# First attention: output parts made pair by pair in a tensor of their own; two output tiles begun in its last pair

## The reference, cut to what matters

```python
qkv = (x @ W_qkv + b_qkv).reshape(b, n, 3, H, D)
q, k, v = (qkv[0], qkv[1], qkv[2])
phi_q = jax.nn.relu(jnp.einsum('bhnd,md->bhnm', q * scale, random_features))
phi_k = jax.nn.relu(jnp.einsum('bhnd,md->bhnm', k * scale, random_features))
kv = jnp.einsum('bhnm,bhnd->bhmd', phi_k, v)
attn = jnp.einsum('bhnm,bhmd->bhnd', phi_q, kv) / M
out = jnp.transpose(attn, (0, 2, 1, 3)).reshape(b, n, c)
return out @ W_proj + b_proj
```

## Time and profile before

| | us |
|---|---|
| median of 3 runs | 1965.44 (1964.88 to 1968.22) |
| profiled execution, its own time | 1962.91 |
| profiled execution, its span | 1961.1 |
| PE busy in it | 1878.2 (96%) |
| DVE busy | 1204.4 (61%) |
| ACT busy | 873.4 (45%) |

### The profile page before, as it was taken

The page is one execution under the profiler, slowest core; times in us unless marked ns, Lnnn a source line. Parts: engine busy times, 40 slices in busy tenths (PEclk is TensorE's granted clock), DMA queues, the critical chain, the costliest instruction groups (busy, mean ns, idle before and its releaser), DMA issues. The chain is left out here.

```text
span 1961.1 us, 32305 instructions
## 1 busy us (share of the span) xinstructions
PE 1878.2 (96%) x13051; PEld 1771.1 (90%) x13051; DVE 1204.4 (61%) x1895; ACT 873.4 (45%) x1176; POOL 94.4 (5%) x96
## 2 busy tenths in 40 slices
PE   5899899999999999998999999899999999999999
PEld 4899799999999999998899999798878888888899
DVE  8467785444333445446557777665666668889732
ACT  6456521222211212224477752424555557777620
POOL 0000000000000000000000100001111101100000
PEclk9999999999999999999999999899999999999999
DMA  3311244121211122110211041425877779999831
GB/s 92 98 46 36 64 115 111 58 72 41 57 57 57 52 69 62 49 49 22 85 33 33 17 154 41 160 89 185 270 240 237 222 227 335 367 378 377 293 118 40
DMA packets 157962, 250.53 MB, mean 128 GB/s; under 512 B 11949, under 2 KB 86189, under 8 KB 157460
## 3 DMA queue, kind: packets, MB, share of 16 engines
q1 hardware_dynamic: 152532, 231.21, 35.5%
q0 software_dynamic: 5040, 17.56, 3.6%
q10 hardware_dynamic: 272, 0.07, 0.0%
HBM read 228.80 MB, written 20.01 MB: 127 GB/s over the span
## 5 line engine op out<-in xcount | busy, mean ns | idle before, releaser
L183 PE MATMUL psum<-products_room 128*128 128x512 f32 (+2 forms) x2160 | 457.8, 366 | 3.2 <-DVE re_credit L3733 2.0
L183 PEld LDWEIGHTS psum<-products_room 128*128 128x128 f32 (+1 forms) x2160 | 388.8, 188 | 47.3 <-issue 2.4
L183 PE MATMUL psum<-ring_hi,xt_sb 128*128 128x256 f32 (+3 forms) x1920 | 354.9, 283 | 9.6 <-PEq L1290 2.8
L3630 DVE TENSOR_TENSOR products_room<-moe_raw,products_room 128x1536 fp32r<-128x1536 f32 x179 | 312.3, 1754 | 77.4 <-ACT products_room L3529 77.0
L3529 ACT ACTIVATE products_room<-moe_raw 128x1536 fp32r<-128x1536 f32 x179 | 266.0, 1489 | 156.2 <-PE psum L183 85.6
L183 PEld LDWEIGHTS psum<-ring_hi,xt_sb 128*128 128x128 f32 (+1 forms) x1920 | 299.5, 188 | 11.4 <-issue 6.3
L183 PE MATMUL psum<-ring_lo,xt_sb 128*128 128x256 f32 (+3 forms) x960 | 270.2, 282 | 0.0
L183 PEld LDWEIGHTS psum<-ring_lo,xt_sb 128*128 128x128 f32 (+1 forms) x960 | 180.2, 188 | 0.0
L183 PE MATMUL psum<-ring_hi,gnn_sb 128*128 128x256 f32 (+1 forms) x810 | 147.5, 283 | 4.5 <-DVE gnn_sb L1191 3.6
L139 DVE TENSOR_TENSOR ring_lo<-ring_raw,ring_hi 128x1536 fp32r<-128x1536 f32 (+1 forms) x64 | 119.4, 1866 | 50.5 <-ACT ring_hi L128 50.4
L191 PE MATMUL psum<-xt_sb,ring_hi 128*128 128x314 f32 x744 | 140.0, 310 | 0.3
(11 more groups left out here) (529 smaller groups left out, 2752.2 us busy)
## 6 DMA issues: line engine op xcount, KB each, us to landing
moe_raw<-in_L_ffn_Wg_r SPq DMA_DIRECT2D x60, 768.0 KB, 5.9
moe_raw<-in_L_ffn_Wu_r SPq DMA_DIRECT2D x60, 768.0 KB, 5.9
moe_raw<-in_L_ffn_Wd_r SPq DMA_DIRECT2D x60, 768.0 KB, 8.6
ring_raw<-in_L_gnn_w_rel SPq DMA_DIRECT2D x18, 896.0 KB, 5.1
ring_raw<-in_L_mix_W_qkv SPq DMA_DIRECT2D x24, 384.0 KB, 4.2
ring_raw<-in_L_gnn_w_rel SPq DMA_DIRECT2D x9, 768.0 KB, 4.7
ring_raw<-in_L_gnn_w_root SPq DMA_DIRECT2D x6, 896.0 KB, 5.1
count_total_dram<-gnn_sb POOLq DMA_DIRECT2D x3, 1570.0 KB, 11.3
```

What stands on the lines that cost most here:

```text
L183: mm = pe.matmul(out, lhs[a], rhs[b], start=(first and i == 0), stop=(last and i == 2))
L3630: dve.tensor_tensor(wlo[:, i % RING, :], raw[i % RAWS], whi[:, i % RING, :].bitcast(F32), ALU.subtract)\
```

## The change

The values of the first attention no longer have a tensor of their own. A new tensor `hidden_sb` (`k.hb`) lives from the start of the program to the end of the graph convolution; it holds first the values, head by head, and then, from its beginning, the parts of the attention's output (`k.at`), each pair's parts over values that are no longer needed. `phase_start` keeps its normalised x in `a_sb`.

In pairs p = 1 to 5 ACT makes the high part of pair p - 1's output behind query block 3, and DVE the low part; only pair 5's own parts are left to the output phase. In pair 5 PE makes, in five groups `lead_tiles(j)`, the products of pairs' parts j = 0 to 4 for row tiles 2 and 3: behind key tiles 3 and 4, behind query blocks 0 and 1, and behind the transposes. `first_tiles` leaves these out. The types, the edges and GpSimd's settings wait for one low part instead of six.

```diff
+AHEAD_TILES = (2, 3)
...
-        vt = k.sb(f"{name}_v", [P, TT, HEADS, vw], F32R)
+        if second:
+            vt = k.sb(f"{name}_v", [P, TT, HEADS, vw], F32R)
+        else:
+            vt = k.hb[:, 0:HEADS * TT * vw].rearrange("p (h t v) -> p t h v", t=TT, v=vw)
...
                     mm.then_inc(s["pk_mm"], 1)
                     project_unit(p + 1, t)
+                    if not second and p == PAIRS - 1 and t >= TT - 2:
+                        lead_tiles(t - (TT - 2))
...
                         for u in range(KD, KD + 3):
                             project_unit(p + 1, u)
+                    if not second and p == PAIRS - 1 and m < 2:
+                        lead_tiles(m + 2)
...
+            def lead_tiles(j):
+                if j == 0:
+                    pe.wait_ge(*st.next.split(0))
+                    pe.wait_ge(s["qk_lo"], qk_count(PAIRS - 1, QUERIES))
+                pe.wait_ge(s["part_lo"], j + 1)
+                for t in AHEAD_TILES:
+                    split_product(pe, k.banks[2 + t][0:TS[t], 0:256], [k.at[:, j, a, t * P:t * P + TS[t]] for a in range(2)],
+                                  [w[:, j, :] for w in st.next.views(0)], j == 0, False)
...
                     turn_values(p, 0)
+                    if p == PAIRS - 1:
+                        lead_tiles(KD - 2)
...
+                    if m == 3 and not second and p >= 1:
+                        act.wait_ge(s["num_f"], 2 * p)
+                        act.activation(k.at[:, p - 1, 0, :], at_f[:, p - 1, :], ACT.Copy).then_inc(s["part_hi"], 1)
...
+                    if m == 3 and not second and p >= 1:
+                        dve.wait_ge(s["part_hi"], p)
+                        dve.tensor_tensor(k.at[:, p - 1, 1, :], at_f[:, p - 1, :], k.at[:, p - 1, 0, :].bitcast(F32), ALU.subtract)\
+                            .then_inc(s["part_lo"], 1)
...
-            sp.wait_ge(s["t_lo"], KD)
+            sp.wait_ge(s["t_lo"], 1)
...
-            pool.wait_ge(s["t_lo"], KD)
+            pool.wait_ge(s["t_lo"], 1)
...
                 for j in range(KD):
-                    pe.wait_ge(s["t_lo"], j + 1)
+                    if j == KD - 1:
+                        pe.wait_ge(s["t_lo"], 1)
                     for t in range(PROJ_BANKS):
+                        if j < KD - 1 and t in AHEAD_TILES:
+                            continue
...
-            for t in range(KD):
-                act.activation(at[:, t, 0, :], at_f[:, t, :], ACT.Copy).then_inc(s["t_hi"], 1)
+            act.activation(at[:, KD - 1, 0, :], at_f[:, KD - 1, :], ACT.Copy).then_inc(s["t_hi"], 1)
...
-            for j in range(KD):
-                dve.wait_ge(s["t_hi"], j + 1)
-                dve.tensor_tensor(at[:, j, 1, :], at_f[:, j, :], at[:, j, 0, :].bitcast(F32), ALU.subtract)\
-                    .then_inc(s["t_lo"], 1)
+            dve.wait_ge(s["t_hi"], 1)
+            dve.tensor_tensor(at[:, KD - 1, 1, :], at_f[:, KD - 1, :], at[:, KD - 1, 0, :].bitcast(F32), ALU.subtract)\
+                .then_inc(s["t_lo"], 1)
...
-        xn = k.sb("n0_xn", [P, TT, D], F32)
+        xn = k.a
```

More of the change, by code:

```diff
@@ L294, in phase_attend @@
             "saved", "rf_in", "chain", "ones_set", "rf_turned", "rf_bd", "rf_hi", "rf_ready", "kn_mm", "kn_f", "v_mm", "v_f", "v_hi",
[L295 removed]
+            "v_lo", "part_hi", "part_lo", "qk_mm", "qk_hi", "qk_lo", "sq_hi", "sq_lo", "pk_mm", "pk_f", "pk_hi", "pk_lo",
             "pq_mm", "pq_f", "pq_hi", "pq_lo", "by_mm", "by_act", "by_dve", "kv_mm", "kv_part", "kv_f", "kv_hi", "kv_lo", "at_mm", "den_f", "num_f",
@@ L914, in phase_project @@
         st = k.streams[name]
-        at = k.gnn[:, RELS * TT * NT:(RELS * TT + 2 * KD) * NT].rearrange("p (j a n) -> p j a n", j=KD, a=2)
+        at = k.at
         at_f = feature_major(k.a)
@@ L1886, in phase_last_layer_ffn @@
         bf = k.sb(f"{name}_bf", [HP, 2], F32)
-        room = k.gnn[:, RELS * TT * NT:]
+        room = k.hb
         cut = np.cumsum([0, 2 * KD * H_FF, 4 * D, 4 * NT]).tolist()
@@ L2456, in gnn_block @@
         k.enter(ctx)
-        k.gnn = k.sb("gnn_sb", [P, (RELS * TT + 2 * K1) * NT], F32R)
-        k.C = k.gnn[:, 0:RELS * TT * NT].rearrange("p (r t n) -> p r t n", t=TT, n=NT)
+        k.C = k.sb("counts_sb", [P, RELS, TT, NT], F32R)
         k.ones = k.sb("ones_r", [P, P], F32R)
@@ L2466, in gnn_block @@
         phase_project(k, "p0", I["src"], I["dst"], I["edge_type_3"], I["L0_gnn_node_emb"], I["node_type_3"])
-        hb = k.gnn[:, RELS * TT * NT:].rearrange("p (j a n) -> p j a n", j=K1, a=2)
+        hb = k.hb[:].rearrange("p (j a n) -> p j a n", j=K1, a=2)
         first = lambda j: k.xt[:, j, :, :]
@@ L4218, in build @@
         k.summed = k.lasting_sem("counts_summed")
[L4219 to L4228, removed]
+        with ExitStack() as graph_ctx:
+            k.enter(graph_ctx)
+            k.hb = k.sb("hidden_sb", [P, 2 * K1 * NT], F32R)
+            k.at = k.hb[:, 0:2 * KD * NT].rearrange("p (j a n) -> p j a n", j=KD, a=2)
+            with ExitStack() as small_ctx:
+                k.enter(small_ctx)
+                k.v_bias = k.sb("v_bias", [P, D], F32)
+                k.out_bias = k.sb("out_bias", [P, D], F32)
+                k.qk_bias = k.sb("qk_bias", [P, 2 * PAIRS], F32)
+                k.features_in = k.sb("features_in", [P, 2, DH], F32)
+                phase_start(k, I["src"], I["dst"], I["edge_type_3"], I["L0_mix_b_qkv"], I["L0_mix_b_proj"],
+                            I["L0_mix_random_features"])
+                phase_attend(k, "m0", False)
+            gnn_block(k, I)
         phase_attend(k, "m1", True, I["L1_mix_random_features"])
```

## The result

The changed kernel takes 1969.34 us (median of 20 runs, 1964.38 to 1971.13), the kernel before 1964.62 (20 runs). The ratio is 1.0023 with a 95% interval of 1.0017 to 1.0030: slower by 4.7 us, 3.3 to 5.9. The forecast was 1969.6. That it is slower is clear of the spread; that it is slower by over 0.2% is not, since the interval reaches down to 0.17%. The profiled execution has a span of 1967.1 us (own time 1968.91).

The account below looks back on a forecast made before the run. The prediction took TensorE (busy 1878.2 of 1961.1 us) as the bound, with only its remaining waits to win. Terms 1.4 + 2.4 - 1.0 + 1.4 = +4.2 us on a median of 1965.4 gave 1969.6 us, range 1964.0 to 1973.0.

Parts of the forecast that it names:

- the likeliest case: Whole kernel: the forecast's own case, between 1967.5 and 1971.5 us, chance 0.52, of which 0.36 lies beyond +0.2%.
- C: Output phase: decoding starts earlier, limited by the landing of the first count rows; -1.0 us, bounds -0.5 and -3.1.
- D: Check of the counts: PE's wait grows to about 4 us and half clock follows; +1.4 us, bounds 0 and 3.4.
- A: Pairs 1 to 4: DVE's low part delays `by_dve` and PE's transposes; +1.4 us, bounds 0 and 2.9.
- B: Last pair: five groups of six matmuls moved in, most not fitting the waits; +2.4 us, 1.3 at full clock.
- landed 5.0 us later: Output phase: the first count rows' transfer, issued at about 232.7, lands at 237.7, letting the first upper digit start 0.6 us earlier.
- a sign of being wrong: Check of the counts: no wait of PE there would show the prediction wrong; it expected one over 3 us.
- Rival 1: Output phase: PE decides there and the groups fit the last pair's waits; -5.5 us, 1959.9 us, chance 0.08.
- Rival 2: Last pair: PE keeps its full clock, so the groups cost 1.3; sum +3.1 us, 1968.5 us, chance 0.14.
- Rival 3: Check of the counts: the clock is kept, or the wait there is shorter; +2.8 us, 1968.2 us, chance 0.14.
- Rival 4: Four pairs and check: DVE's part costs its full 0.72, two slow stretches meet the check; +7.3 us, 1972.7, chance 0.12.

Follow-up runs that it names:

- e3: Changed kernel, but in pairs 1 to 4 ACT and DVE make the parts where they wait for `attend`, not ahead of `by_dve`: 1967.23 us, ratio 1.0015 to before.
- g1: Kernel before with four of DVE's five maximum reductions in the decoding left out: 1963.49 us, ratio 0.9995 to before.
- e4: Changed kernel with the first two loads of count rows issued ahead of the ring's chunk in the output phase: 1967.21 us, ratio 1.0010 to before.
- f1: Changed kernel with the first two count tiles' rows loaded in the last pair, into the free end of `hidden_sb`: 1967.03 us, ratio 1.0011 to before.
- g2: Changed kernel with four of DVE's five maximum reductions in the decoding left out: 1965.07 us, ratio 1.0003 to before.
- e1: Changed kernel without the five groups in the last pair; `first_tiles` makes all its matmuls again: 1964.26 us, ratio 1.0000 to before.
- f2: As f1 (count rows loaded early), but without the five groups in the last pair: 1963.39 us, ratio 0.9991 to before.
- f3: As f2, with the parts of pairs 1 to 4 made where ACT and DVE wait for `attend`: 1962.94 us, ratio 0.9992 to before.
- f4: As f3 (early rows, late parts), but with the groups, placed in the last pair's waits: 1962.74 us, ratio 0.9994 to before.
- e2: Changed kernel with groups 0 and 1 behind query block 1, 2 behind block 2, 3 between the transposes: 1966.46 us, ratio 1.0009 to before.

## Why the prediction was right, and where it was not

**The total.** 1969.3 measured, 1969.6 forecast, and the kernel is slower by over 0.2%, as the likeliest case had it. Two terms came out nearly as worked out; C was 1.3 us too low and D 1.0 too high, and that they nearly made up for one another is luck. So is part of the closeness of the total: the forecast put +4.2 us on a kernel before of 1965.4, and measured were +4.7 on one of 1964.6.

**A, parts ahead of `by_dve`: +1.4 forecast, +1.64 in the trace.** 0.41 us in each of four pairs. The step (copy late by the part's pitch, less the slack that was there) is right, and e3 gives back 1.28 of it.

**B, groups in the last pair: +2.4 forecast, +2.59 between the two profiles.** The wait of about 2 us for the query's last low part came (1.84), the key tile and most of group 1 ran at half clock, and the first query block came 3.46 us late (3.1 forecast; the key tile had been put at 0.86 us, where the earlier trace rows has 1.04). But the last pair of the kernel before is not always 17.58 us: the five other profiles without groups in it have 18.37 to 19.79, g1 among them, whose code is the same up to there. Five profiles with the groups at their first places (changed, e3, e4, f1, g2) have 20.17 to 21.12. By the means, 20.41 and 19.04, the groups cost 1.4 us. The means mix two clocks, though: the pair without groups spent 3.3 to 10.3 us at half clock, 7.4 in the mean, and with them 3.2 to 6.8, 3.9 in the mean. Where it lasted equally long the groups cost 1.8 to 2.7 us (before and e1 against changed, e4, f1 and g2, all at 3.2 to 3.5) and 2.0 (f2 against e3). So the size of the term holds at a like clock, but it was sized on an execution with little half clock; whether the longer stretches come from the missing groups or from chance no run separates.

**C, the output phase: -1.0 forecast, +0.33 measured** (the decoding's end moved by 4.13 us, the phase's start by 3.80). That the landing of the first count rows bounds the gain was right; ACT waited 4.51 us and DVE idled 3.77. The step that failed is "landed 5.0 us later", taken over for the changed kernel: there the first rows took 6.3. e1, which has all of the change but the groups, lands its first rows in 5.0 as before and gets -0.95. So the term was right for the parts, and the groups cost 1.3 us more here than was seen.

**D, the clock at the check: +1.4 forecast, +0.39 measured** (the check began 4.52 us later, the decoding ended 4.13 later)**.** PE did wait over 3 us with half clock behind it, but one tile earlier: at tile 10, for the ring's third chunk, which DVE splits in the middle of its decoding. At the check itself no wait is left, which the prediction had named as a sign of being wrong, and by that sign this step failed: I had read the check as the only meeting point and counted tile 10 among PE's free tiles. Tile 10 then took 3.50 us (260.75 to 264.25) and not 18 x 0.118 = 2.1, the 1.4 us of the forecast. But the decoding ended only at 263.71 (262.91 + 0.80), so the check could not have begun sooner than that, and most of the 1.4 us was spent under it.

The four terms measured make +4.95; less the 0.44 won ahead of pair 0, that is the 4.5 us by which the traces differ at the check. The last 1.5 us of the spans' 6.0 lie behind the start of the check. PE is 1.0 us longer busy there, at a mean granted clock of 0.99 in both profiles; I did not tie it to the change.

**The rivals.** Rival 1 (PE decides in the output phase) is excluded by f1 against f2 and f3 against f4: of 3.5 us of matmuls saved there none and 0.64 us count at the check. Rival 2 (the clock is kept in the last pair): it fell, to 0.50 in 220 to 222 us. There PE had waited 1.27 and 1.84 us with work between, and ran half clock again. In e2, with other waits in the pair, it was kept. The Trainium skill (TensorE: Matmul & The Clock Gate, "What's actually happening") gives the half clock after an idle stretch and the full one after a busy one; read strictly that kept the clock here, and the row decides against that reading. Rival 3 was half right: the clock fell behind tile 10's wait, at less cost. Rival 4 did not come.

## What to carry to other kernels

Work moved into another phase's waits gains only if the engine that does it sets the end of the phase that it left. Look for every place where that engine meets the others, not only the last: here a ring's chunk, split by the decoding engine, stood one tile ahead of the check, and its adds, which free the banks, at every tile. A term sized on one wait of one execution wants a second profile of the same code, since half-clock stretches differ from run to run: this last pair, with the same code, took 17.58 us with 3.5 us of half clock and 19.79 with 10.3.

## What the hardware showed that was not expected

**An instruction fetch in the way of a transfer.** The ring's chunk (768 KB) of the output phase landed after 4.6 to 4.7 us in all six kernels without the groups, and after 5.7 to 6.1 in the seven with them where it was first in the queue, whatever else was changed. The list of DMA queues for a narrow stretch shows one packet of the queue of instructions there. In the changed kernel, 238 to 240 us, 3.3 us behind the issue at 236.11 (packets, MB, share of the 16 DMA engines):

```profile
q8 instruction: 1, 0.02, 3.2%
```

In the kernel before, 240 to 242 us, 8 us behind the issue at 232.30, when the chunk had long landed:

```profile
q8 instruction: 1, 0.02, 4.1%
```

3.2% of 16 engines for 2 us is one engine for 1.0 us, and the landing is 1.3 later. The packet shows 2.3 to 3.3 us behind the issue in the seven with groups, and 6.5, 4.9 and 4.9 in e1, f2 and f3, which land at 4.6. Between the changed kernel and e1, which differ in the groups alone, it moves by 3.2 us, about the 3.5 of the 30 matmuls. The likely reading is that PE, further on in its program, asks for its next instructions earlier: with the 30 of the groups added in, PE had begun 41 to 54 matmuls of the output phase when the packet came, in all 13 profiles. The spread shows that this is not all (e1 and f2 run the same matmuls, and their packets lie 1.6 us apart), and the profile does not name the engine that the packet is for. The Trainium skill (Advanced Engine Details and Errata, "ISA Cache") gives 16 KB as the size of an instruction cache line, and the packet's 0.02 MB agrees. The fit is close over 13 profiles, but no run moves the packet by itself, so this stays an inference.

**Being first in the queue did not make a transfer quick.** The count rows took 5.3 us at the head of the queue with 768 KB right behind them (e4) and 5.2 behind 768 KB (e1); e4 also has an instruction packet 3 us into its transfers, so the two are not alike in all else. Loads of the same rows issued when nothing else ran took about 3.1 (f1).
